# A fused recommendation tower in fp32: layer 0's Gram matrices in 64x64 tiles, H transposed by 64-row transposes, two PSUM slots exchanged

## The reference, cut to what matters

```python
h = inp                                            # (B, 32, 64)
for i, (W, b) in enumerate(zip(Ws, bs)):           # 3 layers of 128 maps
    Wr = W.reshape(O, Hj, nf)
    nxt = jnp.einsum('bjk,bzk,ojz->bok', h, inp, Wr) + b[None, :, None]
    if i != n_layers - 1:
        h, o = (nxt[:, :O // 2], nxt[:, O // 2:])  # half goes on, half goes out
    else:
        o = nxt
    outs.append(o)
z = jnp.sum(jnp.concatenate(outs, axis=1), axis=2) # (B, 256)
h = jnp.concatenate([z, dense_ctx], axis=1)
h = relu(h @ W_top1 + b_top1); h = relu(h @ W_top2 + b_top2); y = h @ W_top3
```

## Time and profile before

| what | value |
|---|---|
| median of 3 runs | 675.24 us (675.22 to 676.35) |
| the profiled execution | 675.91 us, with a span of 674.2 us in the trace |
| TensorE's mean granted clock | 0.98 |
| TensorE matmul (PE) busy | 636.4 us, 94% of the span |
| weight loads (PEld) busy | 508.0 us, 75% |
| VectorE (DVE) busy | 482.4 us, 72% |
| ScalarE (ACT) busy | 215.0 us, 32% |
| GpSimd (POOL) busy | 129.6 us, 19%, none after the lookups end |

### The profile page before, as it was taken

How to read it: one execution, slowest core, us unless ns; L and a number is a source line. 1 busy time by engine, 2 the same in 40 slices (tenths; PEclk the granted TensorE clock), 3 DMA queues, 4 the chain that set the end, 5 groups by cost and what they waited for, 6 DMA issues and landing times.

```text
span 674.2 us, 36102 instructions
## 1 busy us (share of the span) xinstructions
PE 636.4 (94%) x16536; PEld 508.0 (75%) x16536; DVE 482.4 (72%) x490; ACT 215.0 (32%) x351; POOL 129.6 (19%) x137
## 2 busy tenths in 40 slices
PE   5834899999999999999999999999999999999998
PEld 5833668787788888787878787878887878888873
DVE  4237878787888888887888888888888888862000
ACT  2330333344333333433333333333333233333012
POOL 7755034444443543200000000000000000000000
PEclk9686999999999999999999999999999999999999
DMA  5110010001000110000000000000000000002000
GB/s 179 28 27 18 11 26 19 20 21 27 21 21 18 26 23 21 18 11 9 9 8 8 8 8 8 8 8 8 5 6 5 7 8 8 8 8 72 11 2 0
DMA packets 13228, 12.74 MB, mean 19 GB/s; under 512 B 5745, under 2 KB 10465, under 8 KB 12946
## 3 DMA queue, kind: packets, MB, share of 16 engines
q1 hardware_dynamic: 9010, 8.09, 4.6%
q0 software_dynamic: 4192, 4.25, 2.8%
HBM read 8.03 MB, written 0.00 MB: 12 GB/s over the span
## 4 chain that ended last, share of the span: by engine, by line
PE 90%; POOL 5%; issue 3%; DVE 2%; DMA 1%; ACT 0%; DVEq 0%; POOLq 0%
PE psX L325 20%; PE psT L384 19%; PE psT L368 8%; PE psT L408 8%; PE psT L394 7%; PE psT L371 5%; POOL G_sb L229 5%; PE psX L368 5%; PE psX L337 4%; PE psX L371 4%; PE psX L458 2%; PE psX L347 1%; PE psX L263 1%; PE psX L487 1%; DVE PT L709 1%
## 5 line engine op out<-in xcount | busy, mean ns | idle before, releaser
L388 PE MATMUL psT<-T_sb,W1d 64*64 64x256 f32 x1024 | 233.4, 378 | 0.0
L384 PE MATMUL psT<-T_sb,W1d 64*64 64x256 f32 x1024 | 233.4, 378 | 0.0
L394 PE MATMUL psT<-T_sb,W1d 64*64 64x256 f32 (+3 forms) x2048 | 204.4, 299 | 0.0
L673 DVE TENSOR_TENSOR prod<-X 128x1024 f32 (+4 forms) x202 | 170.7, 914 | 18.2 <-PE psT L371 18.1
L709 DVE STREAM_TRANSPOSE PT<-prod 128x4608 f32<-128x4608 f32 x32 | 159.0, 4969 | 0.0
L384 PEld LDWEIGHTS psT<-T_sb,W1d 64*64 64x64 f32 x1024 | 131.4, 133 | 26.3 <-issue 14.1
L325 PE MATMUL psX<-PT,W0T 32*64 32x256 f32 x4608 | 135.5, 382 | 10.1 <-DVE PT L709 9.1
L408 PE MATMUL psT<-T_sb,W1d 64*64 64x64 f32 (+2 forms) x1536 | 141.7, 270 | 0.0
L325 PEld LDWEIGHTS psX<-PT,W0T 32*64 32x64 f32 x4608 | 111.8, 133 | 36.0 <-issue 26.5
L388 PEld LDWEIGHTS psT<-T_sb,W1d 64*64 64x64 f32 x1024 | 131.4, 133 | 0.0
L394 PEld LDWEIGHTS psT<-T_sb,W1d 64*64 64x64 f32 x2048 | 123.7, 133 | 0.8
(11 more groups left out here) (79 smaller groups left out, 569.8 us busy)
## 6 DMA issues: line engine op xcount, KB each, us to landing
X<-T_sb SPq DMA_DIRECT2D x64, 64.0 KB, 1.9
G_sb<-in_L_rec_W SPq DMA_DIRECT2D x2, 1024.0 KB, 6.6
E_q<-in_tbl,ids_g POOLq DMA_INDIRECT x96
prod<-in_W_top SPq DMA_DIRECT2D x2, 512.0 KB, 3.7
G_sb<-in_L_rec_W SPq DMA_DIRECT2D x1, 512.0 KB, 5.8
G_sb<-in_tbl,ids POOLq DMA_INDIRECT x32, 2.4
dT<-dT SPq DMA_DIRECT2D x3, 32.0 KB
zb<-in_L_rec_b SPq DMA_DIRECT2D x4, 0.2 KB
```

The source lines that it names most:

```text
L384: mm(psT[low, 0, 0:HF * SMP], W1d[low, HF + k, :], cross.rearrange("p v (z y) s -> p v z y s", y=HF)[:, :, :, k, :], start=start, stop=sto ...
L388: mm(psT[high, 0, 0:HF * SMP], W1d[low, k, :], T_flat[low, SMP * row:SMP * (row + HF)], start=start, stop=stop, tile_position=(0, C))
L394: last = mm(out[:, SMP * 4 * a:], W1d[high, HF * v + k, :], T_flat[high, SMP * (row + 4 * a):SMP * (row + HF)], start=start, stop=stop and ...
L673: return tt(out, x[:, :, z0:z0 + nz].unsqueeze(3).broadcast_to(shape), x[:, :, y0:y0 + ny].unsqueeze(2).broadcast_to(shape), ALU.mult)
```

## The change

Three edits, and what they need around them:

1. **G0.** `fields` now holds pairs of tiles: one column of ones, 64 field columns (two tiles), one column of ones. `g0_matmuls` has 8 matmuls with 64 weight columns and 66 moving columns. Each gives a 64x66 block that holds two samples' Gram matrices on its diagonal and two cross blocks that nobody needs. `g0_copy` copies all of it to a new buffer `grams`. SyncE moves the wanted blocks to `kept` in four transfers a step, ahead of its two others, in `keep(n)`; a new semaphore `g0_kept` makes the next `g0_copy` and the final contractions wait for them. `kept` has a new layout, in which the words that `z0` reads lie 34 words apart instead of four together.
2. **H.** `h_transposes` has 16 calls of `nc.tensor.transpose`, each of 64 rows and 128 columns, in place of 32 matmuls.
3. **T.** The second and third reuse of slots are exchanged: t = 2 goes to `psT[:, 0:2]` and waits for `g2_copy`, t = 3 to `psX[:, 2:4]` and waits for `g0_copy`. So t = 6 waits for ScalarE's copy of t = 2 where it waited for VectorE's copy of t = 3.

```diff
-NS = NF + 1
+NS = NF + 2
+GRAM = 2 * NF + 2
+ONES = (0, NF + 1)
...
-        fields = sb("fields", [P, 2, TILES, NS])
+        fields = sb("fields", [P, 2, TILES // 2, GRAM])
+        grams = sb("grams", [P, 4, GRAM])
...
-        kept = sb("kept", [P, STEPS, NS * 4])
+        kept = sb("kept", [P, STEPS, 4, NS])
...
-        T_BANKS = [psT[:, 2:4], psX[:, 0:2], psX[:, 2:4], psT[:, 0:2], psT[:, 2:4], psX[:, 0:2], psT[:, 0:2], psT[:, 2:4]]
+        T_BANKS = [psT[:, 2:4], psX[:, 0:2], psT[:, 0:2], psX[:, 2:4], psT[:, 2:4], psX[:, 0:2], psT[:, 0:2], psT[:, 2:4]]
...
-            def keep_g1(n):
+            def keep(n):
+                sp.wait_ge(g0_evac, n + 1)
+                for j in range(4):
+                    r, i = slice(Q * j, Q * j + Q), j % 2
+                    sp.dma_start(kept[r, bass.ds(n, 1), :, i:i + NF + 1],
+                                 grams[r, :, (NF + 1) * i:(NF + 1) * (i + 1)].unsqueeze(1)).then_inc(g0_kept, 16)
                 sp.wait_ge(t_stored, n + 1)
...
-                        for g in range(2):
-                            last = mm(psX[C * g:C * g + C, v, C * t:C * t + C],
-                                      H_sb[r, P * t + C * g:P * t + C * g + C], ident[r, r],
-                                      start=True, stop=True, tile_position=(C * v, C * g))
+                        last = nc.tensor.transpose(psX[:, v, C * t:C * t + C], H_sb[r, P * t:P * t + P], ident[r, r],
+                                                   tile_position=(C * v, 0))
...
-                for t in range(TILES):
+                for pair in range(TILES // 2):
+                    q, g = pair // 2, pair % 2
                     for h in range(2):
-                        x = fields[C * h:C * h + C, e, t, :]
-                        j, q = t % 4, t // 4
-                        last = mm(psX[Q * j:Q * j + Q, 2 + h, NS * q:NS * (q + 1)], x[:, 0:NF], x,
-                                  start=True, stop=True, tile_position=(C * h, Q * j))
+                        x = fields[C * h:C * h + C, e, pair, :]
+                        last = mm(psX[C * g:C * g + C, 2 + h, GRAM * q:GRAM * (q + 1)], x[:, 1:1 + 2 * NF], x,
+                                  start=True, stop=True, tile_position=(C * h, C * g))
...
                     if t == 2:
+                        pe.wait_ge(g2_copied, n + 1)
+                    if t == 3:
                         pe.wait_ge(g0_evac, n + 1)
-                    if t == 3:
-                        pe.wait_ge(g2_copied, n + 1)
                     if t == 4:
                         pe.wait_ge(t_by_act, NA * n + 1)
-                    if t in (5, 6):
-                        pe.wait_ge(t_by_dve, ND * n + t - 4)
-                    if t == 7:
-                        pe.wait_ge(t_by_act, NA * n + 3)
+                    if t == 5:
+                        pe.wait_ge(t_by_dve, ND * n + 1)
+                    if t in (6, 7):
+                        pe.wait_ge(t_by_act, NA * n + t - 4)
...
-                                      W0z[r, HF * v + y, :], kept[r, :, c:c + 4],
+                                      W0z[r, HF * v + y, :], kept[r, :, :, 1 + HF * v + y],
...
                 act.wait_ge(g0_ready, m + 1)
-                copy(kept[:, bass.ds(m, 1), :].rearrange("p n (c q h) -> p (n h) q c", q=2, h=2),
-                     psX[:, 2:4, 0:2 * NS].rearrange("p h (q c) -> p h q c", q=2)).then_inc(g0_evac, 1)
+                act.wait_ge(g0_kept, 16 * 4 * m + 1)
+                copy(grams[:, :, :].rearrange("p (q h) c -> p h q c", h=2),
+                     psX[:, 2:4, 0:2 * GRAM].rearrange("p h (q c) -> p h q c", q=2)).then_inc(g0_evac, 1)
...
+            nc.vector.memset(kept[:, :, :, 0:NS:NS - 1], 0.0)
```

More of the change, by code:

```diff
@@ L147, in dlrm_tower @@
         t_by_act, t_by_dve, t_stored = sem("t_by_act"), sem("t_by_dve"), sem("t_stored")
-        g0_ready, g0_evac = sem("g0_ready"), sem("g0_evac")
+        g0_ready, g0_evac, g0_kept = sem("g0_ready"), sem("g0_evac"), sem("g0_kept")
         g1_sent = sem("g1_sent")
@@ L194, in _ @@
             sp.sem_inc(t_free, 1)
+            sp.sem_inc(g0_kept, 1)
             sp.wait_ge(w_evac, W_BANKS)
@@ L208, in _ @@
             with sp.Fori(0, STEPS - 1) as n:
-                keep_g1(n)
+                keep(n)
             sp.dma_start(Wt1, W_top1[0:2 * P, :].rearrange("(a p) n -> p a n", p=P)).then_inc(late_in, 16)
@@ L214, in _ @@
             sp.dma_start(Wt2, W_top2.rearrange("(a p) n -> p a n", p=P)).then_inc(late_in, 16)
-            keep_g1(STEPS - 1)
+            keep(STEPS - 1)
             sp.wait_ge(y_evac, 1)
@@ L462, in z2 @@
                               V_T[:, j, :],
-                              kept[:, n0:n0 + STEPS // 2, 4 * NF:4 * NS].rearrange("p n (q h) -> p n q h", h=2),
+                              kept[:, n0:n0 + STEPS // 2, :, ONES[j % 2]].rearrange("p n (q h) -> p n q h", h=2),
                               start=False, stop=(j == 3))
@@ L471, in z0 @@
                         for v in range(2):
-                            c = 4 * (HF * v + y)
                             last = mm(Z0_BANKS[j // 2][C * v:C * v + C, j % 2].rearrange("p (n c) -> p n c", c=4),
-                                      W0z[r, HF * v + y, :], kept[r, :, c:c + 4],
+                                      W0z[r, HF * v + y, :], kept[r, :, :, 1 + HF * v + y],
                                       start=(y == 0), stop=(y == HF - 1), tile_position=(Q * j, C * v))
                 return last
+            pe.wait_ge(g0_kept, 16 * 4 * STEPS // 2 + 1)
             z2(0)
             pe.wait_ge(t_by_act, NA * STEPS)
+            pe.wait_ge(g0_kept, 16 * 4 * STEPS + 1)
             z0(0)
@@ L640, in _ @@
             nc.vector.memset(b0_col[C:P, :], 0.0)
+            nc.vector.memset(kept[:, :, :, 0:NS:NS - 1], 0.0)
             nc.vector.memset(V_T[:, :, :], 0.0).then_inc(zeroed, 1)
-            nc.vector.memset(fields[:, :, :, NF:NS], 1.0)
+            nc.vector.memset(fields[:, :, :, 0:GRAM:GRAM - 1], 1.0)
             dve.wait_ge(w0_in, 16)
@@ L685, in x_of @@
             def x_of(e, first_tile):
-                cp(fields[:, e, :, 0:NF], X_fields[:, bass.ds(first_tile, TILES), :])
+                cp(fields[:, e, :, 1:1 + 2 * NF],
+                   X_fields[:, bass.ds(first_tile, TILES), :].rearrange("p (pair i) f -> p pair (i f)", i=2))
                 return cp(by_half[e][:, :, X_AT:HALF], X_halves[:, bass.ds(2 * first_tile, SMP), :])
```

## The result

The changed kernel took **664.97 us** (median of 4 runs, 662.92 to 666.33) beside 675.37 for the kernel before on the same chip: a ratio of 0.9838, 95% interval 0.9818 to 0.9859. The forecast was 664, range 658 to 677. The profiled execution is the slowest of the four, 666.33 us with a span of 664.6.

What follows compares the result with a forecast made beforehand. TensorE's own work was taken to bound every step, counting 31 times. From the profiled 675.91 us, G0 6.4 and H 6.7 less, T 0, tail +1.8 gave 664.6; the median lies 0.67 lower, so 664, range 658 to 677.

Steps and rivals of the forecast that it cites:

- G0: Matmuls before T: no tile-shape change on either side, 0.23 us for 0.44, T 0.21 us earlier per step, 6.4 us.
- the slack that the forecast put at 0.3 us: ScalarE's longer G0 copy, then T's t = 0 copy: 0.3 us of room before t = 4 would wait.
- a gain lost behind ScalarE: Rival at T's t = 4: ScalarE's G0 copy far dearer than bounded, the 0.21 us goes, 670 us; chance 0.12.
- H: H's transposes, row halves side by side: 0.16 us less in 19 steps, 0.31 less in 12 with lookups, 6.7 us.
- The two changes of shape: Into and out of H's transposes: 0.155 us each, from 0.10 of empty array and an unhidden weight load of 0.055.
- The slow load: H's 128-column weight loads at 107 ns: block 1.23 us, no H gain, about 678 us; chance 0.19 shared with halves taking turns.
- The exchange: T's second and third slot reuse swapped: costed at nothing, at most 0.16 us a step, 5 us in all.
- T start, t = 4, its copy, t = 7, loop end does not contain t = 6: Path through T to the next step: t = 6 is not on it, so its earlier start gains nothing.
- VectorE's slack: Before VectorE's first copy of T: idle 0.38 us waiting for TensorE, that slack and no more before VectorE ends last.
- The tail: z0 reading moving words 34 apart: 0.055 us more in each of 32 rounds, +1.8 us, bounds nothing to 3.5.
- the exchange pays in full: Rival at T's end: it, not the loop's end, sets the next step; another 0.13 to 0.16 us per step, 659 us; chance 0.07.
- H in turn: Rival in H: row halves take turns, 16 rounds, block 1.24 us, 678 us; chance 0.19 shared with slow loading, both 0.04.

Runs made afterwards that it cites:

- G0 alone: The kernel before with only G0's 64x64 tiles, its transfers and the new kept layout, T's slots in their old order: 671.40 us, ratio 0.9931.
- the kernel with words in fours: The changed kernel with the four words of a step side by side again in grams and kept, ScalarE's copy writing every fourth word: 659.58 us, ratio 0.9767.
- H in turn: The changed kernel with H's 16 transposes reordered, all 8 of the upper 64 rows before the 8 of the lower: 676.36 us, one run.

## Why the prediction was right, step by step

**G0: right.** Forecast 0.21 us a step, 6.4 us. The gap beside G0 is gone as argued, T begins 0.23 earlier on the mean, and G0 alone shortens the steps by 7.5 us. That the tile shape, and not the halved number of matmuls, is behind it is read from the gap in the timeline; the two were not run apart. What followed G0 kept up: ScalarE's copy takes no longer than before, and the kernel with words in fours shows the slack that the forecast put at 0.3 us: its copy takes 0.28 us more and no step is longer. So the rival of a gain lost behind ScalarE falls at the start of T. It is near at T's end: a delay of 0.15 us of the copy of t = 4 comes through.

**H: right in mechanism, a little large.** Forecast 0.16 and 0.31 a step, 6.7 us; alone it gives 0.12 and 0.31, 5.9. The two halves do work side by side, at 0.062 us a round. The two changes of shape cost what was forecast (0.10 of empty array and a load of some 0.06 on the way out). What was off is the round, 0.062 for 0.058, 0.03 in all, and H before, which was 0.02 cheaper than the 0.93 read from records, since its first records overlapped g2's end. The slow load of the Trainium skill ("TensorE: Matmul & The Clock Gate", section "LDWEIGHTS (loading the stationary operand)", 107 ns for 128 columns) does not hold for these transposes: a round of 0.062 has one 128-column load in each row half.

**The exchange: costed at nothing, worth 1 to 2 us.** The step that failed is "the chain T start, t = 4, its copy, t = 7, loop end does not contain t = 6". It was read from the end of one step, an even one, and it holds there: TensorE's branches end last, and T's earlier end is lost. In the odd steps of the kernel before, T's stream, with t = 6 in it, ended last. The exchange moved that by 0.12 us, and 0.06 of it counted before VectorE's copy of t = 5 ended last in its place: 0.03 on the mean of two steps without lookups. The forecast looked for VectorE's slack at its first copy of T, where 0.22 us are left, and not at its last, for which the next step waits. With lookups the exchange gains 0.11 to 0.12. Why more than without is not settled: without the exchange T also starts 0.10 us later in every second one of those steps. The rival that the exchange pays in full, 0.13 to 0.16 in each step, falls.

**The tail: the mis-sized term.** Forecast +1.8 us with an upper bound of 3.5; measured +4.3, outside the bound, and 32 x (0.24 - 0.11) = 4.2 by `z0`'s rounds alone. The nearest row, strided weights at 0.64 ns a word, was the wrong measure. The forecast took two streams of 128 words one after the other, 0.165 us a round; the round of 0.24 is 0.94 ns a word by that count. By the words of one stream it is 0.24 / 128 = 1.9 ns, and 0.11 / 128 = 0.86 where they are contiguous. The kernel with words in fours took it all back, so the layout is the cause. The Trainium skill, "SBUF — State Buffer", section "Specifications (TRN2)", gives lines of 16 bytes that want two hits each for full bandwidth. Four fp32 words fill one, a word in 34 is one hit. The trace agrees in direction: 0.11 us against 0.24 a round.

**The sum.** 14.5 us from the steps less 4.3 of tail is 10.2, and the medians differ by 10.4; the forecast had 11.3. The steps gave 1.4 us more than forecast (alone, G0 gives 1.1 more, H 0.8 less, the exchange 2.0 more, or 1.3 by the kernel without it), and that hid over half of the tail's error of 2.5. So the total, right to 1 us, owes something to luck: two errors of opposite sign.

**The rivals.** H in turn was made, and its one run gives 676.36, by 13 rounds in place of the 16 that the rival assumed. It did not happen in the changed kernel because the halves' transposes alternate in its order.

## What to carry to other kernels

Read the cost of a small TensorE block from what stands before and after it: here the empty array and the exposed load of a change of tile shape (0.10 and 0.06 us) are a fifth of a block of 0.80, and by the timeline much of G0's gain comes from having no such change. When a layout is changed for its writer, price its readers by a stride of the same kind of operand; keeping the reader's words in fours gave 4.2 us on top of the change. Read an engine's slack at the work that the next stage waits for, in each kind of step: VectorE had 0.22 us at T's first copy and none at its last in one step of two. And weigh an edit by the steps of one profile, not by medians alone, where the first steps vary by 3 us.

## What the runs showed of the hardware that was not expected

- A strided moving operand (words 34 apart) streams at 1.9 ns a word, more than double the contiguous 0.86, at full clock.
- ScalarE writes strided words dearly too: 264 words took 0.39 us to contiguous places and 0.67 to every fourth one, 1.06 ns a word more. That would explain why twice the words cost no more than the 0.41 us of before, which was strided: by the two contiguous copies (640 words in 0.71, 264 in 0.39) 132 contiguous words would take an estimated 0.27 us, and 132 x 1.06 ns is 0.14 more.
- Sixteen transposes of two row halves, one half after the other in the program, took 13 rounds of 0.062 us: three times two of them ran side by side. Alternating, they took 8.
- A loop body twice as long cost stalls of 3.55 and 3.75 us without a semaphore behind them, with packets on the instruction queue at the same time, and after one a granted clock of 0.84 for 21 us, where an undisturbed step has 1.00.
- A branch is not free on TensorE's path: a jump over one copy of G0 and T took 0.17 us, in every second step.
